# Products that nobody reads, put into TensorE's waits of a two-layer gated cross-attention kernel

## The reference

```
x += tanh(g_xattn[0]) * attention(layernorm(x), ctx)        # 16 heads of 16; keys: 120 context rows + 256 own rows
x += tanh(g_ffn[0])   * ternary(layernorm(x))               # ONE scale for the whole tensor: max|layernorm(x)| / 127
x += tanh(g_xattn[1]) * (rmsnorm(layernorm(x)) @ W_in + b_in + recurrence(ctx)[plug])
x += tanh(g_ffn[1])   * int8(layernorm(x))                  # a scale per row and one per weight column
```

## Time and profile before

| | us |
|---|---|
| median of 3 runs (1152.93 to 1156.45) | 1152.98 |
| the profiled execution, whole | 1152.34 |
| its span, first to last instruction | 1150.5 |
| TensorE busy | 1062.2 |
| VectorE busy | 937.9 |
| ScalarE busy | 815.3 |
| GpSimd busy | 693.4 |

### The profile page before, as it was taken

One profiled execution on the slowest core, in us unless ns is written; L12 is line 12 of the kernel. 1 busy time (PEld: TensorE's weight loads), 2 busy tenths in 40 slices (PEclk: granted clock), 3 DMA queues, 4 the chain that ended last, 5 costly groups with the idle time before them and its releaser, 6 DMA issues.

```text
span 1150.5 us, 33448 instructions
## 1 busy us (share of the span) xinstructions
PE 1062.2 (92%) x8458; PEld 711.5 (62%) x8458; DVE 937.9 (82%) x2332; ACT 815.3 (71%) x1730; POOL 693.4 (60%) x1255
## 2 busy tenths in 40 slices
PE   5789999999999999999999999999999959988885
PEld 3356666666666666666666666666665537777773
DVE  5867878878888788888888887887777857999997
ACT  3167777777777777777777777777776648888773
POOL 6455555666655666666666666555555127778776
PEclk9799999999999999999999999999999988999997
DMA  4433333333334333343334344334333101222222
GB/s 140 118 88 103 102 106 104 99 99 99 99 100 113 101 103 105 104 106 103 106 105 107 102 105 105 104 101 107 93 97 83 47 27 44 81 80 80 87 89 91
DMA packets 158680, 110.18 MB, mean 96 GB/s; under 512 B 17154, under 2 KB 154788, under 8 KB 158628
## 3 DMA queue, kind: packets, MB, share of 16 engines
q1 hardware_dynamic: 158356, 109.30, 35.1%
q10 hardware_dynamic: 272, 0.26, 0.1%
HBM read 30.30 MB, written 16.29 MB: 40 GB/s over the span
## 4 chain that ended last, share of the span: by engine, by line
PE 61%; DVE 13%; issue 8%; SPq 6%; POOL 5%; DMA 4%; ACT 1%; DVEq 1%; POOLq 0%; ACTq 0%
PE pv_ps L676 14%; PE ms_ps L661 13%; PE st_ps L651 12%; PE misc L699 9%; PE misc L707 3%; SPq L424 3%; SPq L422 3%; DVE neg L897 3%; DMA q<-negT 2%; PE misc L702 2%; PE aux L723 2%; PE aux L728 1%; DVE am L1281 1%; DVE xs L1270 1%; PE misc L691 1%
## 5 line engine op out<-in xcount | busy, mean ns | idle before, releaser
L897 DVE TENSOR_REDUCE neg<-ms_ps 128x1 f32<-128x376 f32 x1024 | 527.4, 544 | 165.5 <-PE ms_ps L661 158.0
L991 ACT ACTIVATE probs<-st_ps 128x512 f32<-128x512 f32 x768 | 428.7, 598 | 34.9 <-PE st_ps L651 30.2
L661 PE MATMUL ms_ps<-k,q 96*128 96x376 bf16 x1024 | 334.6, 328 | 23.1 <-DVE neg L897 18.6
L651 PE MATMUL st_ps<-q,k 99*128 99x256 bf16 x1536 | 294.6, 273 | 6.4 <-DMA q<-negT 5.7
L651 PEld LDWEIGHTS st_ps<-q,k 99*128 99x128 bf16 x1536 | 136.5, 98 | 127.1 <-issue 39.6
L676 PE MATMUL pv_ps<-probs,v 128*32 128x256 f32 (+1 forms) x3072 | 193.9, 385 | 0.0
L699 PE MATMUL misc<-xnT,wqkvT 128*128 128x256 f32 x512 | 155.6, 388 | 2.6 <-ACT xnT L1017 1.9
L661 PEld LDWEIGHTS ms_ps<-k,q 96*128 96x128 bf16 x1024 | 98.6, 96 | 93.0 <-DVE neg L897 59.1
L513 POOL TENSOR_SCALAR negp<-neg 128x16 bf16<-128x16 f32 x64 | 13.1, 205 | 196.8 <-DVE neg L897 196.8
L676 PEld LDWEIGHTS pv_ps<-probs,v 128*32 128x32 f32 (+1 forms) x3072 | 87.3, 110 | 69.5 <-issue 23.4
L699 PEld LDWEIGHTS misc<-xnT,wqkvT 128*128 128x128 f32 x512 | 92.9, 196 | 7.8 <-ACT xnT L1017 2.8
(11 more groups left out here) (188 smaller groups left out, 1834.5 us busy)
## 6 DMA issues: line engine op xcount, KB each, us to landing
k<-parts SPq DMA_DIRECT2D x384, 94.0 KB, 2.7
q<-parts SPq DMA_DIRECT2D x384, 64.0 KB, 2.4
out_dram<-xn SPq DMA_DIRECT2D x32, 256.0 KB, 2.2
xs<-in_x SPq DMA_DIRECT2D x31, 256.0 KB, 2.8
cx<-in_ctx SPq DMA_DIRECT2D x32, 240.0 KB, 2.9
recurrence_input<-u_in SPq DMA_DIRECT2D x32, 120.0 KB, 2.3
plug<-plugs SPq DMA_DIRECT2D x32, 120.0 KB, 3.5
powers<-gath SPq DMA_DIRECT2D x32, 120.0 KB, 1.9
```

Of the source, the lines that this page charges most:

```text
L651: mm = pe.matmul(st_ps[u % SR][:, j * S:(j + 1) * S], k6[0:KM, r, h, k * P:(k + 1) * P], q6[0:KM, r, h, :], start=True, stop=True)
L661: pe.matmul(ms_ps[t][:, 0:KEYS], q6[0:KR, r, h % HU, t * P:(t + 1) * P], k6[0:KR, r, h % HU, 0:KEYS], start=True, stop=True).then_inc(s_ms, 1)
L897: dve.tensor_reduce(neg[:, m, t, h % HU:h % HU + 1], ms_ps[t][:, 0:KEYS], AX.X, ALU.max, negate=True).then_inc(s_red, 1)
L991: act.activation(probs[:, u % PR, :], st_ps[u % SR][:, :], ACT.Exp).then_inc(s_exp, 1)
```

## The change

TensorE gets more products. `busy(pe, bank, n)` issues n products of `onesb` (128 x 128, bf16, all ones) with itself, broadcast to 512 columns, into a whole bank. Nothing reads the result, no semaphore is raised, and no product has a wait of its own. They go to the following places.

- At the start: 8 after `onesb` is set (TensorE now waits for 7 constants, not 4), 2 after the transposes of the qkv weights, 5 at the start of `setup` (after iteration -2), 3 each ahead of units 1, 2 and 8 of iteration -2.
- In iteration -1: 2 ahead of every unit except unit 5, and 16 ahead of unit 5, that is, ahead of the last part of the q projection.
- In iteration 32: 4 ahead of each of the units 2, 4, 6 and 14.
- Between the stages and in the row stage: 24 ahead of the transpose of the maxima (L1164), 2 ahead of the spreading product (L1166), 8 after it, 8 more after the scales are there (`s_glob` 13), and 4 at the start of TensorE's part of each of the row iterations 0 to 8 (`MM2` is 9).

```diff
-        N_IDENT = 4
+        N_ONES = 7
+        def busy(pe, bank, n):
+
+            for _ in range(n):
+                pe.matmul(bank[:, :].rearrange("p (r c) -> p r c", c=P), onesb[:, :], onesb[:, :].unsqueeze(1).broadcast_to([P, 4, P]),
+                          start=True, stop=True)
+
         def tensor_attention(pe):
 
-            pe.wait_ge(s_const, N_IDENT)
+            pe.wait_ge(s_const, N_ONES)
+            busy(pe, ms_ps[0], 8)
             pe.wait_ge(d_qkv, 16)
...
             mm.then_inc(s_set_pe, 1)
+            busy(pe, ms_ps[0], 2)
 
             def setup():
+                busy(pe, ms_ps[0], 5)
                 pe.wait_ge(d_proj, 16)
...
                     first, *others = maxima_of(u)
+                    if isinstance(b, int) and b == -2 and u in (1, 2, 8):
+                        busy(pe, ms_ps[0], 3)
+                    if isinstance(b, int) and b == -1:
+                        busy(pe, ms_ps[0] if u < 5 else st_ps[2], 16 if u == 5 else 2)
+                    if isinstance(b, int) and b == LAST and u in (2, 4, 6, 14):
+                        busy(pe, st_ps[2], 4)
                     if live(b):
                         scores_t(u)
...
         def tensor_rows(pe):
+            busy(pe, st_ps[2], 24)
             pe.wait_ge(s_glob, 5)
             pe.transpose(misc[0:1, 0:P], am1[:, 0:1], ident[:, :]).then_inc(s_glob, 1)
+            busy(pe, st_ps[2], 2)
             pe.wait_ge(s_glob, 7)
             pe.matmul(misc[:, P:P + 1], ones[0:1, :], row1[:, 0:1], start=True, stop=True).then_inc(s_glob, 1)
+            busy(pe, st_ps[2], 8)
             pe.wait_ge(s_glob, 13)
+            busy(pe, st_ps[2], 8)
             pe.wait_ge(s_row, ROW_DONE)
...
+                if isinstance(n, int) and n < MM2:
+                    busy(pe, st_ps[2], 4)
                 if live(n - MM1):
```

## The result

| | before | changed |
|---|---|---|
| median of nine runs, us | 1152.93 | 1158.55 |
| ratio, 95% interval | 1 | 1.0051, 1.0037 to 1.0064 |
| profiled execution, us | 1152.34 | 1158.55 |
| its span, us | 1150.5 | 1156.8 |
| mean granted clock | 0.976 | 0.991 |

The change is slower by 0.5%, with more clock granted. The forecast had 1157.2 for the median, in a range of 1151.5 to 1161, and 1156.5 for the profiled execution.

What follows compares the result with a forecast made beforehand. It took TensorE as the bound from 954.35 to 971.64, VectorE from 986.33, the seam as a chain of short steps. Row stage +4.6 (tail included) and start -0.4 gave +4.2: 1156.5 profiled, 1157.2 median, range 1151.5 to 1161.

Steps and rivals of the forecast that it cites:

- The price: Each added 512-column product costs TensorE 0.218 us at full clock, bounds 0.16 and 0.43.
- rival A: Everywhere: products cost less than their columns, so the clock's gain shows; 1147.8 us if nearly free; chance 0.15.
- The tail: Iteration 32, last batch: two groups of fillers stand ahead of L723, which starts 1.07 us late.
- The seam: Between the stages: 28 products take 6.1 us where 2.79 was idle; the row stage's first transposes come 3.0 late.
- The ramp: Row iterations up to 9: full clock shortens steps, fillers lengthen them; iteration 9's transposes come 4.7 us late.
- the start: Iterations -3 to -1: small gains and losses together give -0.4 us, bounds -1.5 and +5.
- at about 1.6 us a unit behind it: Iteration -1, units 20 to 23: VectorE is the bound, TensorE's work stays behind it; the last unit's fillers lose 0.4.
- cost nothing: Start, ahead of the first maxima: the added products end near 27.9, before 29.11, covered by a 4.08 us wait.
- rival C: Start: clock still low at the sixteen, so first maxima and all behind come up to 5 us late; 1161; chance 0.1.
- Iteration 1: Nothing is added there; if other timing avoided its clock fall, about 1.5 us gained, kept for the range.
- rival B: Forecast's ramp, but more clock gain at the start and no fall in iteration 1: +2.1, 1155; chance 0.2.

Runs made afterwards that it cites:

- start_only: The change with only the added products of iterations -3 to -1, tail, seam and row products dropped; median 1158.93 us, ratio 1.0028 to the kernel before.
- no_6to8: The change without the groups at row iterations 6, 7 and 8, run twice; 1159.88 and 1158.75 us, ratios 1.0055 and 1.0048 to the kernel before.
- seam_fit: The change with 12 instead of 28 products between L1183 and the row stage's first transposes; 1158.52 us, ratio 1.0038 to the kernel before.
- after_again: The changed kernel, unedited, run again on another chip; median 1162.17 us, ratio 1.0075 to the kernel before.
- before_again: The kernel before, unedited, run and traced a second time; median 1154.20 us, ratio 0.9992 to the kernel before.

## Why the prediction was right, and which term was not

**The price.** Predicted 0.218 us a product; the 24 of the seam start 0.2155 apart (5.34 us with the last one's own length, 0.38), a pair at the low clock takes 0.96 us against 0.54 at the full one. The row decides, and with it rival A is out. The prediction's 2.4 and 1.2 GHz are its names for the granted clock, of which the traces show the share alone, 1.00 and 0.50. At 0.50 two products of 512 columns start 0.427 us apart (start_only at 24.04: 1.06 us with the last one's own 0.63), 1.2 columns a nanosecond; at 1.00 it is 2.4. As gigahertz they are an estimate from these two, with one column a cycle.

**The tail.** Predicted +1.07, measured +1.08 or +1.09 in six traces.

**The seam.** Predicted 2.8 behind the tail (3.9 in all), measured 2.91 to 2.94 in five traces; with twelve instead of 28, -0.29. L1195 starts 7.01 us after L1180; 6.9 was said.

**The ramp.** Predicted 4.7 up to iteration 9, counted from the last attention product; measured 1.08 + 2.91 - 1.05 + 1.73 = 4.67. The iterations were said to be 5.3 us apart and are 5.28. VectorE's gapless stretch hands this on to the end, give or take the row loop's two modes (below).

**Two slips in the working.** The earlier trace rows has TensorE at nine tenths from the fourth slice to the thirty-second, not from the second to the thirty-first; slices 2 and 3 are at seven and eight. Rival A's slope, by its own two points (4.6 at 0.218, 1.3 at 0.16), is 57 and not 55 us per us, with the crossing at 0.137. Neither changes the forecast.

**The sum's undersized term was the start.** Predicted -0.4. start_only has +3.3 by the median. The step that failed is the one on the units behind the first maxima: VectorE "is the bound", with TensorE "at about 1.6 us a unit behind it". It priced every pair at the full clock, 0.44. Where the clock falls among them a pair costs 0.96, and it stands ahead of the maxima in TensorE's order. From the first maxima to iteration 0 it took 25.2 us in the traces that had these pairs and kept the clock up (both of no_6to8), 26.5 to 28.1 where it fell, and 24.8 to 25.6 without the pairs, although the clock was low for part of that (0.50 from 38.1 to 48.2 in before). So even at their best they gained nothing. Where the clock stayed full the step held: a loss of 0.3 behind the one-hot rows, a gain of 0.3 ahead of them. The step "cost nothing" for the sixteen held in the changed kernel's traces, and failed in those of start_only and seam_fit (first maxima at 31.62 and 31.32): that is rival C in part, 2.2 to 2.5 us of its 5.

**Iteration 1.** Kept out of the sum and kept for the range. The fall was gone in the change's first trace, which is half of rival B's mechanism (its larger gain at the start did not come); but it came back in after_again (0.50 from 85.8 to 89.0), and the kernel before lacked it in before_again. The wait that rival B names stands ahead of the fall in the trace of before, 2.02 us up to L651 at 81.27 with 0.50 from 82.5 to 85.8; before_again has 2.03 us up to 82.79 and no fall (1.00 from 80.8 to 86.0). The six traces with the fall have a wait of 1.9 to 2.9 us ahead of it, four have one of 2.0 to 2.3 and no fall, the other four none above 1.65 and no fall: the wait goes with the fall and doesn't settle it. It belongs to the execution. Likewise the fall in iteration 31, +1.58 in the change's trace, absent in that of after_again.

So the nearness of 1156.5 to the 1158.55 of the profiled execution is in part luck. Against the forecast's +4.2 its trace has 2.5 us more up to iteration 0, 1.4 less in iterations 0 and 1, 2.8 more from there to the last value products (1.6 of it the fall in iteration 31), 0.1 more from there to iteration 9, and 2.0 less behind it, together 2.0. When the change was run again, it was 1.0075, 9.1 us above before; the two intervals hardly touch. The places where the clock falls and the row loop's two modes (below) are what differs between the traces, and how often each comes was not measured.

Left open: drifts of up to 1.5 us within iterations 2 to 30 that vary between executions; why the clock falls in iteration 1 or 31 in some executions; where the start's pairs lose the part of their 4.5 us that the traces don't locate.

## What to carry to other kernels

Products that keep the clock up are work like any other: they cost their columns (0.216 us for 512), in order, in front of whatever stands behind them. Count the idle of each place in the trace and put in no more than it holds; the same idea cost 5.6 us here, 3.2 of it by 28 products in a place that holds twelve, and gained 5.6 when they were counted. Put none where TensorE is in the chain of waits or a little behind it: when the clock falls anyway, they cost about twice as much (0.96 us a pair here, not 0.43 to 0.54).

## What the runs showed of the hardware that was not expected

The row loop has two modes. A pair of iterations takes 6.0 + 5.8 us or 6.3 + 5.9, and the number of 6.3s in a trace was 4 and 8 in the two of before, 0 and 6 in the two of the change, 0 to 8 in the others. That is 0.4 us a pair, and most of the up to 3.6 us by which the ledger's rows behind iteration 9 differ. The timeline of before, VectorE and GpSimd, first in the short mode, then in the long one:

```profile
1013.94 1.44 POOL L1133 TENSOR_TENSOR xn<-xs,v 128x256 f32<-128x256 f32 x2 [0.45 <-issue]
...
1014.64 0.15 DVE L1288 TENSOR_SCALAR ls<-am 128x2 f32<-128x2 f32 x1
...
1025.75 1.41 POOL L1133 TENSOR_TENSOR xn<-xs,v 128x256 f32<-128x256 f32 x2 [0.45 <-issue]
...
1026.45 0.73 DVE L1288 TENSOR_SCALAR ls<-am 128x2 f32<-128x2 f32 x1
```

The same tiny instruction takes 0.15 or 0.73 us, and in both cases GpSimd's second addition of L1133 starts with it. Taken one by one over all fourteen traces, with every L1288 that starts within 0.06 us of such an addition: in the 62 short ones the addition's record starts at most 0.022 us ahead (or 0.004 behind), in the 64 long ones 0.010 to 0.031 us ahead. All above 0.022 are long, and the two kinds overlap between 0.010 and 0.022. In each trace there are as many long ones as 6.3s. So it is a tie of some hundredths of a microsecond that decides 0.6 us on VectorE, the bound there. The lengths go with it: the 64 long ones take 0.72 to 0.74 us, as the addition does (0.72 to 0.74), and end 0.02 to 0.03 us behind it; the 62 short ones take 0.14 to 0.15 beside an addition of 0.73 to 0.76. What holds L1288 up isn't shown: no trace names a cause. No experiment here moved the tie; that it can be won for good by a changed order was not tried.
